# Attention output products ahead of the raw scores, and the queries' rotation in two pieces

## The chip, the cores and the metric

The program runs on one core of a Trainium2 chip. TensorE does the matrix products (PE in the profile; its weight loads are PEld), VectorE (DVE) the elementwise work and maxima, ScalarE (ACT) exponentials and copies out of PSUM, GpSimd (POOL) elementwise work in SBUF, SyncE (SP) issues DMAs. The metric is the device time of one execution in microseconds (us), the median of several.

## The reference

Four layers on x of 8 sequences x 256 tokens x 128 features, each `x = x + layer(layernorm(x))`: attention with rotary embedding ("rope"), a transformer block with a mixture of experts ("ffn"), attention whose scores are a covariance plus a variance term ("cov"), and the same ffn block again. All attentions have 16 heads of 8 features. Cut to its core:

```
rope: q, k, v = rot(x Wq.T + bq), rot(x Wk.T + bk), rot(x Wv.T + bv)
      out = unrot(softmax(q k.T / sqrt(8)) v) Wo.T + bo
cov:  softmax((q - mean(q)) (k - mean(k)).T / 8 + var(q) var(k).T / 8) v Wo.T
ffn:  h = x + attention(layer_norm(x)); h + moe(layer_norm(h)), top 2 of 8 experts, hidden 512
rot(x1, x2) = [x1 cos - x2 sin, x1 sin + x2 cos]      x1, x2: even and odd features
```

All data is float32.

## The kernel before, in words

Everything stays in SBUF. The two halves of the program (ph 0 and 1) each take two layers: first an attention pipeline over 16 items, an item being one sequence in one layer (rope then ffn in ph 0, cov then ffn in ph 1), then `mixture`, the experts over all tokens.

The pipeline goes in steps. In one step each engine works on up to six items that stand at different stages, called u, t, a, m, n, p from the oldest to the youngest. n is projected to queries, keys and values, and these are turned to feature-major (`do_zT`, `do_proj`, `do_kT`, `do_qT`). m gets its raw scores, `do_raw` (line 370), two heads at a time, of which VectorE takes the row maxima (`do_max`, line 982); the maxima are turned (`do_mT`, line 394) and sent by DMA into a spare row of the turned queries as a shift. a gets the shifted scores the other way round, `do_scores` (line 357), of which ScalarE takes the exponentials (`do_exp`, line 729), and the products of these with the values, `do_pv` (line 384). t's output is turned (`do_outT`, line 454), divided on VectorE (`divide`, lines 992 and 996), for rope rotated back on GpSimd, turned and multiplied by Wo. u is normalised and turned for the gate (`do_uT`, line 482).

A step on TensorE has eight slots, 0 to 7. Slot i has `do_scores` of heads 2i and 2i+1 of a, then `do_raw` of heads 2i-2 and 2i-1 of m, then transposes or other small products, then a `do_pv`. The order of each engine's instructions is that of the code; engines meet at semaphores alone. I write S for a `do_scores` of two heads, R for a `do_raw` of two heads, PV for a `do_pv`.

The features of four heads lie on the 128 partitions, 32 to a head, so a score product of head h uses only the 32 rows of TensorE's array at 32 * (h % 4): a strip. Heads 2i and 2i+1 of a slot's S are on two strips, and the R beside it, one pair of heads behind, is on the other two. PV uses all rows but 32 columns of the array for each of four heads.

S and the transposes write into a ring of four banks that ScalarE empties, R and the projections into a ring of three banks that VectorE empties. An R has to wait until the maxima of the heads three ring places before are taken; S for exponentials; `do_pv(g, ..)` for all four exponentials of the group g.

On VectorE a rope item n is rotated by two products for each of keys (1), queries (0) and values (2): `rotate` (lines 966 and 967), with the order of the calls written out in `step`. GpSimd adds the two products (`rotated`, line 1280) and lays keys and queries out for the transposes (`stack_k`, `stack_q`).

Of the kernel before, what the change touches and what calls it, by code (L numbers as in the profile page):

```python
# [7 lines left out]
ALU = mybir.AluOpType  # L8
# [95 lines left out]
def build(nc, d, out):  # L104
    ctx = ExitStack()
    with ctx:
        def sb(name, shape, dt=F32):
            return ctx.enter_context(nc.sbuf_tensor(name, shape, dt))
# [10 lines left out]
        def event(name, per):  # L119
            return Event(sem(name), per)  # L120
# [24 lines left out]
        ropeA = sb("ropeA", [P, 3, TT, H, HD])  # L145
        ropeB = sb("ropeB", [P, 3, TT, H, HD])
# [9 lines left out]
        QKV = sb("QKV", [P, 3, TT, D])  # L156
        R1 = sb("R1", [P, 3, TT, H, HD])
        R2 = sb("R2", [P, 3, TT, H, HD])
# [60 lines left out]
        roped = event("roped", {"rope": 6})  # L219
# [56 lines left out]
        def dve_bank(*key):  # L276

            return bankR[:, ring_r.place[key]]
# [63 lines left out]
        def _(pe):  # L342
# [6 lines left out]
            def do_scores(layer, b, i):  # L349

                if i % 4 == 0:
                    need(pe, shifted[i // 4], layer, b)
                for h in (2 * i, 2 * i + 1):
                    ring_e.take(pe, ("S", layer, b, h))
                    rows, kb, g = head_rows(layer, b, h)
                    for z in range(TT):
                        k = mm(act_bank("S", layer, b, h)[:, z * T:z * T + T], KT[rows, kb, g, z * P:z * P + P],  # L357
                               QT[rows, kb, g, :], start=True, stop=True)
                    k.then_inc(scores.sem, 1)
                    ring_e.give(("S", layer, b, h), exped, layer, b, h + 1)  # L360
# [14 lines left out]
            def do_pv(layer, b, g, kc):  # L375
                need(pe, exped, layer, b, HG * g + HG)
                if (g, kc) == (0, 0):
                    need(pe, stacked, layer, b)
                    need(pe, pv_copied, layer, b, 0)
                if (g, kc) == (2, 0):  # L380
                    need(pe, pv_copied, layer, b, 1)
                cols = slice((g // 2) * T, (g // 2) * T + T)
                for j in range(HG):
                    k = mm(bankO[SL * j:SL * j + SL, cols], Vx[:, b % VB, kc, HG * g + j, :],  # L384
                           Pr[:, g % 2, j, kc, :], start=(g % 2 == 0 and kc == 0),
                           stop=(g % 2 == 1 and kc == TT - 1))
                if kc == TT - 1:
                    k.then_inc(pv.sem, 1)
# [117 lines left out]
            def step(u, t, a, m, n, p):  # L506
                if a:
                    do_scores(*a, 0)
                    do_raw(*a, 7)
                if n:  # L510
                    do_zT(*n)
                if t:
                    do_pv(*t, 3, 0)

                if a:
                    do_scores(*a, 1)
                if m:
                    do_raw(*m, 0)
                if a:
                    do_mT(*a, 1)  # L520
                if t:
                    do_pv(*t, 3, 1)
                if n:
                    do_proj(*n)

                if a:
                    do_scores(*a, 2)
                if m:
                    do_raw(*m, 1)
                if a:  # L530
                    do_pv(*a, 0, 0)

                if a:
                    do_scores(*a, 3)
                if m:
                    do_raw(*m, 2)
                if t:
                    do_outT(*t)
                if m == (0, 0):
                    do_fold()  # L540
                if a:
                    do_pv(*a, 0, 1)

                if a:
                    do_scores(*a, 4)
                if m:
                    do_raw(*m, 3)
                if u:
                    do_uT(*u)
                if a:  # L550
                    do_pv(*a, 1, 0)

                if a:
                    do_scores(*a, 5)
                if m:
                    do_raw(*m, 4)
                if n and LAYERS[n[0]] != "rope":
                    do_kT(*n)
                if a:
                    do_pv(*a, 1, 1)  # L560

                if m:
                    do_mT(*m, 0)
                if a:
                    do_scores(*a, 6)
                if m:
                    do_raw(*m, 5)
                if u:
                    do_gate(*u)
                if t:  # L570
                    do_onT(*t)
                if n:
                    if LAYERS[n[0]] == "rope":
                        do_kT(*n)
                    else:
                        do_qT(*n)
                if a:
                    do_pv(*a, 2, 0)

                if a:  # L580
                    do_scores(*a, 7)
                if m:
                    do_raw(*m, 6)
                if t:
                    do_wo(*t)
                if n and LAYERS[n[0]] == "rope":
                    do_qT(*n)
                if a:
                    do_pv(*a, 2, 1)
# [300 lines left out]
        def _(dve):  # L890
            v = nc.vector
            tt = v.tensor_tensor
# [53 lines left out]
            def rope_operands(ap):  # L946
                half = ap.rearrange("p n (w o) -> p n w o", o=2)
                n = ap.shape[1]
                ev = half[:, :, :, 0].unsqueeze(2).broadcast_to([P, n, 2, HD // 2])
                od = half[:, :, :, 1].unsqueeze(2).broadcast_to([P, n, 2, HD // 2])  # L950
                return ev, od

            def flat(ap):
                return ap.rearrange("p c t h (u w) -> p (c t h) u w", u=2)

            def heads(ap):

                return ap.rearrange("p c t (h x) -> p (c t h) x", x=HD)

            def rotate(layer, b, c):  # L960

                need(dve, proj_copied, layer, b)
                if (layer, b, c) == (0, 0, 1):
                    dve.wait_ge(in_rope2, 4 * 16)
                ev, od = rope_operands(heads(QKV[:, c:c + 1]))
                tt(flat(R1[:, c:c + 1]), ev, flat(ropeA[:, c:c + 1]), ALU.mult).then_inc(roped.sem, 1)
                tt(flat(R2[:, c:c + 1]), od, flat(ropeB[:, c:c + 1]), ALU.mult).then_inc(roped.sem, 1)  # L967

            def turn(layer, b, part):
                if LAYERS[layer] == "cov":  # L970
# [8 lines left out]
            def do_max(layer, b, i):  # L979
                for h in (2 * i, 2 * i + 1):  # L980
                    need(dve, raw, layer, b, h + 1)
                    v.tensor_reduce(M[:, b % 2, :, h], dve_bank("raw", layer, b, h).rearrange("p (t k) -> p t k", t=TT),  # L982
                                    AX.X, ALU.max, negate=True).then_inc(maxed.sem, 1)
# [49 lines left out]
            def step(gone, u, t, a, m, n, nxt):  # L1033
                if a:
                    do_max(*a, 7)
                if m:
                    do_max(*m, 0)
                rope = n and LAYERS[n[0]] == "rope"
                if n:
                    do_proj(*n)  # L1040
                if m:
                    do_max(*m, 1)
                if n:
                    turn(*n, 0)
                if rope:
                    rotate(*n, 1)
                if m:
                    do_max(*m, 2)
                if n:
                    turn(*n, 1)  # L1050
                if rope:
                    rotate(*n, 0)
                if t:
                    divide(*t)
                if m == (0, 0):
                    do_fold()
                if m:
                    do_max(*m, 3)
                if m:
                    do_max(*m, 4)  # L1060
                if u:
                    rest_of_u(*u)
                if nxt:
                    norm_in(*nxt)
                if m:
                    do_max(*m, 5)
                if rope:
                    rotate(*n, 2)
                if u:
                    do_gate(*u)  # L1070
                if block_of(gone) is not None:
                    weigh(*block_of(gone))
                if block_of(u) is not None:
                    choose(*block_of(u))
                if m:
                    do_max(*m, 6)
                if t:
                    residual(*t)
                    norm3_in(*t)
# [419 lines left out]
```

## Time and profile before

| | |
|---|---|
| Time before, median of 3 runs | 1014.32 us (1014.15, 1014.32, 1019.89) |
| Profiled execution, its own time | 1015.21 us |
| Its span in the trace | 1013.4 us |
| Busy in the span | PE 96%, PEld 72%, ACT 60%, DVE 56%, POOL 37% |
| Matmuls | 8418 |
| Mean granted TensorE clock, share of full | 0.984 |

The span is the stretch of the trace from the first instruction to the last; the profiled execution took 1.81 us more than its span. A busy share of PE counts matmuls whose ends are modelled, overlapping ones included. Times in the trace count from the start of the span.

### The profile page before, as it was taken

Reading aid. Unit: us, or ns where it says so; the run is one execution under the profiler, and the core shown is the slowest. Engines: PE = TensorE matmul, PEld = TensorE weight load, DVE = VectorE, ACT = ScalarE, POOL = GpSimd, SP = SyncE. Lnnn points to the kernel's source line nnn. Section 1 sums busy time; section 2 is a strip of 40 time slices with the busy share of each in tenths; the row PEclk is TensorE's granted clock in tenths of the full one; section 3 lists DMA queues with packets and bytes.
Section 4 is the critical chain, followed back from the end, with each engine's and each line's share of the span. In section 5 each row is a group of like instructions: output and inputs, shape, how many; then the busy total and the mean of one; then the engine's idle time right before and its main releaser. Section 6 shows DMA issues by size and latency. Waiting matters only on the chain.

```text
span 1013.4 us, 22026 instructions
## 1 busy us (share of the span) xinstructions
PE 970.4 (96%) x8418; PEld 731.9 (72%) x8418; DVE 563.2 (56%) x1434; ACT 604.5 (60%) x1144; POOL 374.1 (37%) x797
## 2 busy tenths in 40 slices
PE   2989999999999999999999999999999999999998
PEld 2655556666557999999886666666665799999997
DVE  4797887888982221222336878788898222121211
ACT  1376668878787444444355777787878745444343
POOL 6768777657721100013112446366771110000000
PEclk9998889999999999999999999999999999999999
DMA  9000000000000000000000000000000000000000
GB/s 287 9 3 2 3 2 3 3 3 3 3 3 2 1 2 1 1 1 1 2 1 2 3 3 3 3 3 3 3 3 3 2 1 12 1 11 2 7 6 11
DMA packets 9960, 10.42 MB, mean 10 GB/s; under 512 B 1528, under 2 KB 7552, under 8 KB 9856
## 3 DMA queue, kind: packets, MB, share of 16 engines
q1 hardware_dynamic: 8848, 7.64, 2.6%
q10 hardware_dynamic: 1008, 1.38, 0.5%
q8 instruction: 68, 1.11, 0.4%
q14 instruction: 36, 0.29, 0.1%
HBM read 7.44 MB, written 1.05 MB: 8 GB/s over the span
## 4 chain that ended last, share of the span: by engine, by line
PE 78%; DVE 17%; issue 2%; POOL 1%; DMA 0%; ACT 0%; DVEq 0%; ACTq 0%; POOLq 0%
PE bankR L613 23%; PE bankO L384 10%; DVE M L982 8%; PE bankE L403 8%; PE bankE L602 6%; PE bankE L357 6%; PE bankE L604 6%; PE bankE L603 6%; PE bankR L370 3%; DVE QKV L944 2%; PE bankE L394 2%; PE bankR L454 1%; PE bankR L424 1%; PE bankR L472 1%; DVE R L967 1%
## 5 line engine op out<-in xcount | busy, mean ns | idle before, releaser
L982 DVE TENSOR_REDUCE M<-bankR 128x2 f32<-128x512 f32 x512 | 326.3, 684 | 70.2 <-PE bankR L370 68.4
L729 ACT ACTIVATE Pr<-bankE 128x512 f32<-128x512 f32 x512 | 276.9, 594 | 108.1 <-PE bankE L357 105.8
L839 ACT ACTIVATE Pr<-bankE,b1c 128x512 f32<-128x512 f32 x256 | 171.1, 687 | 175.4 <-PE bankE L604 174.2
L1138 DVE SCALAR_TENSOR_TENSOR X<-bankR,WE,X 128x128 f32<-128x128 f32 x256 | 72.1, 344 | 327.5 <-PE bankR L613 327.5
L613 PEld LDWEIGHTS bankR<-w,Pr 128*128 128x128 f32 x2048 | 238.3, 192 | 6.3 <-issue 1.1
L613 PE MATMUL bankR<-w,Pr 128*128 128x128 f32 x2048 | 238.9, 276 | 0.9 <-DVE X L1138 0.9
L370 PE MATMUL bankR<-KQ 32*128 32x256 f32 x1024 | 170.4, 340 | 10.6 <-DVE On L996 3.7
L384 PE MATMUL bankO<-Pr,Vx 128*32 128x256 f32 x2048 | 166.1, 398 | 0.6 <-ACT OT L721 0.3
L357 PEld LDWEIGHTS bankE<-KQ 32*128 32x128 f32 x1024 | 81.0, 188 | 96.0 <-issue 61.8
L357 PE MATMUL bankE<-KQ 32*128 32x256 f32 x1024 | 134.4, 334 | 0.0
L370 PEld LDWEIGHTS bankR<-KQ 32*128 32x128 f32 x1024 | 109.5, 192 | 23.3 <-DVE M L982 12.9
L602 PE MATMUL bankE<-THL,w1h 128*128 128x512 f32 x256 | 106.9, 417 | 0.0
L604 PE MATMUL bankE<-THL,w1l 128*128 128x512 f32 x256 | 101.1, 395 | 0.0
L603 PE MATMUL bankE<-THL,w1h 128*128 128x512 f32 x256 | 100.9, 394 | 0.0
L1222 POOL TENSOR_SCALAR lnsmall<-meanvar 128x2 f32<-128x2 f32 x48 | 10.9, 228 | 236.2 <-DVE meanvar L912 233.7
L721 ACT ACTIVATE KQ<-bankE 128x512 fp32r<-128x512 f32 x128 | 70.8, 604 | 24.2 <-PE bankE L403 23.9
L384 PEld LDWEIGHTS bankO<-Pr,Vx 128*32 128x32 f32 x2048 | 41.1, 109 | 35.4 <-issue 12.0
L1297 POOL CAST Kst<-QKV 128x512 fp32r<-128x512 f32 x24 | 16.2, 674 | 134.3 <-DVE QKV L942 93.0
L604 PEld LDWEIGHTS bankE<-THL,w1l 128*128 128x128 f32 x256 | 48.1, 188 | 11.9
L602 PEld LDWEIGHTS bankE<-THL,w1h 128*128 128x128 f32 x256 | 48.3, 189 | 10.2
L603 PEld LDWEIGHTS bankE<-THL,w1h 128*128 128x128 f32 x256 | 48.3, 189 | 8.7
L403 PE MATMUL bankE<-ident_r,Kst 128*128 128x256 f32 (+1 forms) x256 | 43.0, 319 | 4.1 <-POOL Kst L1300 4.1
(157 smaller groups left out, 1137.3 us busy)
## 6 DMA issues: line engine op xcount, KB each, us to landing
THL<-in_w SPq DMA_DIRECT2D x1, 2048.0 KB, 9.1
KQ<-MT SPq DMA_DIRECT2D x128, 4.0 KB
X<-in_x SPq DMA_DIRECT2D x8, 128.0 KB, 7.3
out_x<-X SPq DMA_DIRECT2D x4, 256.0 KB, 2.3
ropeA<-in_ropeA ACTq DMA_DIRECT2D x1, 384.0 KB, 5.9
ropeB<-in_ropeB ACTq DMA_DIRECT2D x1, 384.0 KB, 6.0
w_lo_rope<-in_w_qkv_rope ACTq DMA_DIRECT2D x1, 192.0 KB, 3.0
b_qkv_rope<-in_b_qkv_rope ACTq DMA_DIRECT2D x1, 192.0 KB, 4.9
```

The costliest lines, as they stand in the source:

```text
L357: k = mm(act_bank("S", layer, b, h)[:, z * T:z * T + T], KT[rows, kb, g, z * P:z * P + P], QT[rows, kb, g, :], start=True, stop=True)
L370: k = mm(dve_bank("raw", layer, b, h)[:, z * T:z * T + T], QT[rows, kb, g, z * P:z * P + P], KT[rows, kb, g, :], start=True, stop=True)
L384: k = mm(bankO[SL * j:SL * j + SL, cols], Vx[:, b % VB, kc, HG * g + j, :], Pr[:, g % 2, j, kc, :], start=(g % 2 == 0 and kc == 0), stop=( ...
L403: return mm(bank[:, i * P:i * P + n], src, ident_r[:, 0:n], start=True, stop=True)
L602: mm(acc, w1h[:, e, w], th, start=True, stop=False)
L603: mm(acc, w1h[:, e, w], tl, start=False, stop=False)
L604: mm(acc, w1l[:, e, w], th, start=False, stop=True).then_inc(hid.sem, 1)
L613: k = mm(dve_bank("out", ph, at)[:, t * D:t * D + D], G[:, e % 2, c, t * P:t * P + P], w2[:, e * FC + c, :], start=(c == 0), stop=(c == FC ...
L729: nc.scalar.activation(Pr[:, (h // HG) % 2, h % HG], act_bank("S", layer, b, h).rearrange("p (k q) -> p k q", k=TT), ACT.Exp, scale=EXP_SC ...
L839: nc.scalar.activation(G[:, e % 2, c, :], act_bank("hid", ph, at, c), ACT.Gelu_apprx_tanh, bias=b1c[:, e * FC + c:e * FC + c + 1]).then_in ...
L982: v.tensor_reduce(M[:, b % 2, :, h], dve_bank("raw", layer, b, h).rearrange("p (t k) -> p t k", t=TT), AX.X, ALU.max, negate=True).then_in ...
L1138: v.scalar_tensor_tensor(xt[:, j, t, :], dve_bank("out", ph, at)[:, t * D:t * D + D], WE[:, j * BT + t, e:e + 1], xt[:, j, t, :], ALU.mult ...
```

## The change

On TensorE, in slots 2 to 5 of each step, `do_pv` of item a is issued directly behind `do_scores`, and so ahead of `do_raw` of item m and of the transposes. On VectorE, `rotate` now does one of its two products per call; keys' and values' two products stay together where they were, while the queries' two go apart: the first behind `do_max(m, 3)`, the second behind `do_max(m, 4)`, where before both stood ahead of `divide` and `do_max(m, 3)`. The instructions on ScalarE and SyncE stay in their order, and so do those of GpSimd.

```diff
@@ TensorE, step
                 if a:
                     do_scores(*a, 2)
+                if a:
+                    do_pv(*a, 0, 0)
                 if m:
                     do_raw(*m, 1)
-                if a:
-                    do_pv(*a, 0, 0)
 
                 if a:
                     do_scores(*a, 3)
+                if a:
+                    do_pv(*a, 0, 1)
                 if m:
                     do_raw(*m, 2)
...
@@ VectorE
-            def rotate(layer, b, c):
+            def rotate(layer, b, c, x):
 
                 need(dve, proj_copied, layer, b)
                 if (layer, b, c) == (0, 0, 1):
                     dve.wait_ge(in_rope2, 4 * 16)
-                ev, od = rope_operands(heads(QKV[:, c:c + 1]))
-                tt(flat(R1[:, c:c + 1]), ev, flat(ropeA[:, c:c + 1]), ALU.mult).then_inc(roped.sem, 1)
-                tt(flat(R2[:, c:c + 1]), od, flat(ropeB[:, c:c + 1]), ALU.mult).then_inc(roped.sem, 1)
+                own, table = ((R1, ropeA), (R2, ropeB))[x]
+                tt(flat(own[:, c:c + 1]), rope_operands(heads(QKV[:, c:c + 1]))[x], flat(table[:, c:c + 1]),
+                   ALU.mult).then_inc(roped.sem, 1)
...
@@ VectorE, step
                 if n:
                     turn(*n, 1)
-                if rope:
-                    rotate(*n, 0)
                 if t:
                     divide(*t)
                 if m == (0, 0):
                     do_fold()
                 if m:
                     do_max(*m, 3)
+                if rope:
+                    rotate(*n, 0, 0)
                 if m:
                     do_max(*m, 4)
+                if rope:
+                    rotate(*n, 0, 1)
                 if u:
                     rest_of_u(*u)
```

The order that results on TensorE, slots 2 to 5 of the first step in which item t exists, before (S is line 357, R 370, PV 384, the transposes of `do_outT` 454, of `do_mT` 394):

```order
L357 MATMUL bankE<-KQ 128x256 x4
L370 MATMUL bankR<-KQ 128x256 x4
L384 MATMUL bankO<-Pr,Vx 32x256 x4
L357 MATMUL bankE<-KQ 128x256 x4
L370 MATMUL bankR<-KQ 128x256 x4
L454 MATMUL bankR<-ident,OT 128x128 x4
L384 MATMUL bankO<-Pr,Vx 32x256 x4
L357 MATMUL bankE<-KQ 128x256 x4
L370 MATMUL bankR<-KQ 128x256 x4
L384 MATMUL bankO<-Pr,Vx 32x256 x4
```

The same place now:

```order
L357 MATMUL bankE<-KQ 128x256 x4
L384 MATMUL bankO<-Pr,Vx 32x256 x4
L370 MATMUL bankR<-KQ 128x256 x4
L357 MATMUL bankE<-KQ 128x256 x4
L384 MATMUL bankO<-Pr,Vx 32x256 x4
L370 MATMUL bankR<-KQ 128x256 x4
L454 MATMUL bankR<-ident,OT 128x128 x4
L357 MATMUL bankE<-KQ 128x256 x4
L384 MATMUL bankO<-Pr,Vx 32x256 x4
L370 MATMUL bankR<-KQ 128x256 x4
```

PV has moved from behind R to between S and R; each R now has a PV ahead of it and the next slot's S (or transposes) behind it.

VectorE in a rope step with an item t, from the rotation of the keys on, before (line 982 the maxima, 966 and 967 the rotation products, 992 and 996 the division, 909 and 912 the statistics of the next item):

```order
L966 TENSOR_TENSOR R<-QKV,ropeA 128x256
L967 TENSOR_TENSOR R<-QKV,ropeB 128x256
L982 TENSOR_REDUCE M<-bankR 128x2 x2
L966 TENSOR_TENSOR R<-QKV,ropeA 128x256
L967 TENSOR_TENSOR R<-QKV,ropeB 128x256
L992 RECIPROCAL rden<-bankR 128x32
L996 TENSOR_TENSOR On<-bankR,rden 128x4x32 x2
L982 TENSOR_REDUCE M<-bankR 128x2 x4
L909 BN_STATS stats<-X 128x6 x2
L912 BN_AGGR meanvar<-stats 128x2 x2
```

The same place now (both products of `rotate` have line 966):

```order
L966 TENSOR_TENSOR R<-QKV,ropeA 128x256
L966 TENSOR_TENSOR R<-QKV,ropeB 128x256
L982 TENSOR_REDUCE M<-bankR 128x2 x2
L992 RECIPROCAL rden<-bankR 128x32
L996 TENSOR_TENSOR On<-bankR,rden 128x4x32 x2
L982 TENSOR_REDUCE M<-bankR 128x2 x2
L966 TENSOR_TENSOR R<-QKV,ropeA 128x256
L982 TENSOR_REDUCE M<-bankR 128x2 x2
L966 TENSOR_TENSOR R<-QKV,ropeB 128x256
L909 BN_STATS stats<-X 128x6 x2
```

The division and the maxima of slot 4 moved ahead of the queries' products, and each of these stands behind a pair of maxima.

## Rows read from the trace of the kernel before

**Rows 1.** The page's first part: busy time, share and count by engine.

```profile
PE 970.4 (96%) x8418; PEld 731.9 (72%) x8418; DVE 563.2 (56%) x1434; ACT 604.5 (60%) x1144; POOL 374.1 (37%) x797
```

**Rows 2.** Stretches of steps: length, busy PE, PEld, DVE, ACT, POOL, then clock, DMA.

```profile
62.99:160.88 97.89, 91.64 (x844) 56.49 (x840) 80.88 (x164) 64.83 (x131) 75.82 (x135) 0.86 0.01 2
160.88:223.15 62.27, 61.41 (x677) 38.33 (x673) 51.81 (x109) 50.33 (x106) 41.05 (x88) 1.00 0.01 3
223.15:289.42 66.27, 64.98 (x705) 41.43 (x701) 58.23 (x155) 52.42 (x115) 43.33 (x98) 1.00 0.01 3
...
557.88:643.34 85.46, 83.55 (x845) 52.19 (x841) 70.25 (x141) 63.52 (x131) 46.85 (x114) 0.98 0.01 3
```

**Rows 3.** TensorE, slots 2 to 5, ffn item n, no u: start, us, instruction, idle.

```profile
193.19 0.39 PE L357 MATMUL bankE<-KQ 32*128 32x256 f32 x2
...
193.42 0.28 PE L357 MATMUL bankE<-KQ 32*128 32x256 f32 x2
...
193.88 0.64 PE L384 MATMUL bankO<-Pr,Vx 128*32 128x256 f32 x8
194.45 0.39 PE L357 MATMUL bankE<-KQ 32*128 32x256 f32 x2
...
195.25 0.63 PE L454 MATMUL bankR<-ident,OT 128*128 128x128 f32 x4 [0.19 <-DVE M L982]
...
196.38 0.39 PE L357 MATMUL bankE<-KQ 32*128 32x256 f32 x2
...
197.41 0.39 PE L357 MATMUL bankE<-KQ 32*128 32x256 f32 x2
...
198.23 1.15 PE L403 MATMUL bankE<-ident_r,Kst 128*128 128x256 f32 x8
...
199.87 0.27 PE L394 MATMUL bankE<-ident,M 128*8 128x128 f32 x1
```

**Rows 4.** TensorE where no item m is left: S stands alone.

```profile
305.89 0.50 PE L357 MATMUL bankE<-KQ 32*128 32x256 f32 x4
306.32 0.44 PE L482 MATMUL bankE<-ident,U 128*128 128x128 f32 x2
306.69 0.64 PE L384 MATMUL bankO<-Pr,Vx 128*32 128x256 f32 x8
```

**Rows 5.** TensorE, slots 2 to 5 of an ffn step with an item u.

```profile
240.97 0.39 PE L357 MATMUL bankE<-KQ 32*128 32x256 f32 x2
...
247.65 0.38 PE L394 MATMUL bankE<-ident,M 128*8 128x128 f32 x2
```

**Rows 6.** VectorE in the last rope step.

```profile
142.50 1.29 DVE L982 TENSOR_REDUCE M<-bankR 128x2 f32<-128x512 f32 x2
...
146.66 0.63 DVE L966 TENSOR_TENSOR R<-QKV,ropeA 128x256 f32<-128x256 f32 x1
...
148.09 0.34 DVE L992 RECIPROCAL rden<-bankR 128x32 f32<-128x32 f32 x1
...
148.87 2.48 DVE L982 TENSOR_REDUCE M<-bankR 128x2 f32<-128x512 f32 x4
```

**Rows 7.** TensorE in the same step, slot 5 and behind it.

```profile
149.01 1.39 PE L370 MATMUL bankR<-KQ 32*128 32x256 f32 x4 [0.55 <-DVE On L996]
...
151.34 0.59 PE L394 MATMUL bankE<-ident,M 128*8 128x128 f32 x2
```

**Rows 8.** TensorE in a cov step: start of slot 2, and behind slot 5.

```profile
575.96 0.39 PE L357 MATMUL bankE<-KQ 32*128 32x256 f32 x2
...
583.97 0.38 PE L394 MATMUL bankE<-ident,M 128*8 128x128 f32 x2
...
584.30 0.39 PE L370 MATMUL bankR<-KQ 32*128 32x256 f32 x2
```

**Rows 9.** VectorE in the same cov step.

```profile
576.57 1.29 DVE L982 TENSOR_REDUCE M<-bankR 128x2 f32<-128x512 f32 x2
...
584.90 1.29 DVE L982 TENSOR_REDUCE M<-bankR 128x2 f32<-128x512 f32 x2 [0.66 <-PE bankR L370]
```

More of the change, by code:

```diff
@@ L530, in step @@
                 if a:
-                    do_pv(*a, 0, 0)
+                    do_scores(*a, 3)
                 if a:
-                    do_scores(*a, 3)
+                    do_pv(*a, 0, 1)
                 if m:
@@ L541, in step @@
                 if a:
-                    do_pv(*a, 0, 1)
+                    do_scores(*a, 4)
                 if a:
-                    do_scores(*a, 4)
+                    do_pv(*a, 1, 0)
                 if m:
@@ L550, in step @@
                 if a:
-                    do_pv(*a, 1, 0)
+                    do_scores(*a, 5)
                 if a:
-                    do_scores(*a, 5)
+                    do_pv(*a, 1, 1)
                 if m:
@@ L558, in step @@
                     do_kT(*n)
-                if a:
-                    do_pv(*a, 1, 1)
                 if m:
@@ L1045, in step @@
                 if rope:
-                    rotate(*n, 1)
+                    rotate(*n, 1, 0)
+                    rotate(*n, 1, 1)
                 if m:
@@ L1067, in step @@
                 if rope:
-                    rotate(*n, 2)
+                    rotate(*n, 2, 0)
+                    rotate(*n, 2, 1)
                 if u:
```

## The prediction

> **What bounds the kernel now.** I read the page first: TensorE is busy 96% of the span, no other engine over 60% [rows 1]. That share alone proves little, since matmuls overlap in it, so I then cut the attention pipeline at the projections of successive steps [rows 2]. The four stretches of the rows are 5 rope steps (97.89 us, 19.58 each), 4 steps that load an ffn item but have no item u (62.27, 15.57 each), 4 with both (66.27, 16.57 each), and 5 cov steps (85.46, 17.09 each). The second half of the program repeats the two ffn kinds in the same number, and each half ends with one further step with u and m. In the ffn steps TensorE is busy nearly throughout at full clock and VectorE has 3 us free in each: (62.27 - 51.81) / 4 = 2.6. In the rope steps the mean clock is 0.86, VectorE is busy 80.88 of 97.89, and TensorE is seen waiting: an R of slot 5 stands idle until the division is done [rows 7]. So ffn steps are set by how long TensorE's own blocks take, rope steps by VectorE in slots 3 to 5, and cov steps stand between.
>
> **What a slot costs on TensorE.** This is the view on which I rest most. In slot 2 of an ffn step S starts at 193.19 and PV at 193.88; PV then takes until 194.45, which is 0.57 [rows 3]. S and R together, eight products, so take 0.69, and in slot 4, where nothing waits, 197.41 - 196.38 - 0.57 = 0.46. Where no item m is left and S stands alone with half as many products, it takes 306.32 - 305.89 = 0.43 [rows 4]. R beside S is thus almost free, 0.03 us. The reason can be seen in the starts: S's second pair of products starts 0.23 behind its first pair [rows 3], one pair on two strips, the next on the same two strips once the first is through. R uses the other two strips in the same 0.46. The change puts PV, which uses all rows, between S and R. And the S that now follows R without anything between is that of the next slot: R has heads 2i-2 and 2i-1, S heads 2i+2 and 2i+3, four apart, so on the same two strips as R. That pair goes one behind the other. I cost every S and every R of slots 2 to 5 at 0.43 of its own.
>
> The Trainium skill, TensorE: Matmul & The Clock Gate, Part 3, says that a weight load overlaps running matmuls only where it goes to another row group; by that rule the trace agrees, in the 0.23 between products of one strip. TensorEngine Tiling (Array Packing), Key Properties, has the rule that a change of tiling mode drains the array. Read as the only cost of the new order, it would charge for one or two more mode changes in a step and not for the lost company on the strips, a few tenths of a microsecond per step; that would be the second rival below.
>
> **ffn steps.** Before, the S and R blocks of slots 2 to 5 take, waits included, 0.69, then 195.25 - 194.45 = 0.80, then 0.46, then 198.23 - 197.41 = 0.82: 2.77 in all [rows 3]. After, eight blocks of 0.43 are 3.44. The four PVs, the transposes of the output and of the keys are the same in number and cost. Per step that is +0.67. The stretch with an item u is as long, 247.65 - 240.97 = 6.68 [rows 5] against 199.87 - 193.19 = 6.68 [rows 3], though it holds a transpose more, 306.69 - 306.32 = 0.37 [rows 4]. Its S and R blocks are then 2.77 - 0.37 = 2.40, and the change costs it 3.44 - 2.40 = +1.04. There are 4 steps of the first kind in each half and 5 of the second (4 and the last with an m): 8 x 0.67 + 10 x 1.04 = 5.4 + 10.4 = +15.8 us. Counted in this are the waits which the new order takes away: of R for a bank in slots 2, 3 and 5, together 2.77 - 4 x 0.46 = 0.93, now covered by PV. The cover holds if VectorE keeps up. An R now reaches an idle VectorE 1.00 (S and PV) + 0.60 (from the start of R to the maxima, 584.90 - 584.30 [rows 8, 9]) = 1.60 into slot 2, where before the maxima began at 576.57 - 575.96 = 0.61 [rows 8, 9]. VectorE is 1.0 later there, but TensorE's slots have grown by as much two slots on, and its 2.6 us of free time is enough. I add nothing; a bound is the whole 0.99 once per step, which would make these terms 18 x 0.99 = 18 us dearer, but nothing in the rows points to more than a tenth or two.
>
> **cov steps.** Here VectorE is at work without a gap from slot 2's maxima to behind slot 5's: its next wait is ahead of the maxima of slot 6 [rows 9]. So its 1.0 us later start goes through to the last R of slot 5, and to the keys' transposes behind it. The transposes of the maxima, 583.97 before [rows 8], then come 0.98 later, less the 0.57 of a PV that no longer stands ahead of them: +0.41. Six such steps (the five of the rows and one ahead of them) make +2.5. Bounds: -0.5 per step if VectorE had slack that I don't see, +1.0 if the PV saves nothing.
>
> **rope steps.** In the row's step the maxima of slot 2 start at 142.50, the queries' products at 146.66, the division at 148.09, the maxima of slots 4 and 5 at 148.87, and the transposes of the maxima at 151.34 [rows 6, 7]. Now the maxima of slot 2 start 0.98 later (as above), but the queries' two products, 148.09 - 146.66 = 1.43, are gone from ahead of the division. So division at 147.64 and slot 4's maxima at 148.42; two maxima take half of the four's 2.4, so they are through at 149.6, and the transposes of the maxima can follow at 149.7, 1.65 earlier. What is given back: the first of the queries' products, some 0.45, now lies ahead of slot 5's maxima, on which the R of slot 6 waits. The second ends near 151.7, where GpSimd had both by 148.1; but GpSimd is busy rotating the output back then, and the queries are transposed only in slot 7, so I price that at nothing, and at 0.5 if GpSimd is late. That leaves 1.2 per step for the five steps with a t, -6.0. Shorter waits also mean fewer stretches at half clock. A mean of 0.86 [rows 2] means that 28% of the 97.89 us, 27 us, ran at the 1.2 GHz level; on TensorE's path alone full clock would give back half of that, 13.7, but much of it lies in waits on VectorE. I take 2.5. Rope together: -8.5, between +5 (1.0 later per step, and nothing won by the moved products) and -15. The first rope steps, which lack an a or a t, I leave at nothing.
>
> **The sum.** 15.8 + 2.5 - 8.5 = +9.8, against the profiled execution's 1015.2: 1025.0. The median before is 0.9 lower, so by difference 1024.1; with a tenth per ffn step for VectorE's lateness I say 1025. The mixture stages have no slot of this kind, and get nothing.
>
> **The rivals.** (1) The rope steps gain nothing: VectorE's later start in slot 2 cancels the moved products and the clock falls as before. For it: VectorE's 80.88 busy of 97.89, and the price of 1.0 per step is sure. Against it: 1.43 leaves the chain in which TensorE is seen to wait. Time: 1015.2 + 18.3 + up to 3 = 1033 to 1036. (2) The strips cost nothing, PV in front of R hides R's waits and only those show: faster. Then R and the next S share 0.46 as before, the stretch of slots 2 to 5 has six blocks of about 0.45, 2.7 against 2.77 and 2.40, some +2.4 over the 18 ffn steps; with the rope gain of 8.5 to 15 and cov at 0 to 2.5 the end is 1003 to 1010. It decides if two products on one strip could overlap; their 0.23 distance speaks against it. (3) The rope gain is whole, with the clock at full: -13 to -15 there, 1018 to 1021. For it: each low-clock stretch follows a wait that gets shorter. (4) VectorE becomes the bound of the ffn steps as well, by several tenths per step: 1030 to 1040. The 2.6 us free speak against it. That the change doesn't do what it says can be left out: the order of both engines shows it.
>
> **How the numbers follow.** Forecast (1021 to 1030) 0.50, rival 1 with the upper part of the sum 0.18, rival 3 0.20, rival 4 0.06, rival 2 0.06. The range 1017 to 1035 leaves out rival 2 and the ends of 1 and 4. A difference under 1%, 10.1 us, counts as none that can be told, so slower begins at 1024.5, near the middle of the forecast: 0.30 of its 0.50, all of rivals 1 and 4, 0.54; faster only by rival 2, 0.06; the same 0.40.
>
> **What would show it.** In the changed profile an S of slots 2 to 5 alone should take 0.43 to the PV, an R followed by S 0.86 to 0.88; ffn steps should be 16.2 to 16.3 and 17.6 long, cov steps 17.2, rope steps 17.5 to 18.5 with a clock above 0.86. VectorE's first maxima should start 1.6 into slot 2. The prediction is wrong if R with the next S takes under 0.6, or if rope steps stay at 19.6.

## The result and the profile after

The changed kernel takes 1033.84 us (median of 4, 1029.37 to 1035.05) against 1017.11 us of the kernel before on the same chips (median of 4, 1014.15 to 1020.18): ratio 1.0168, 95% interval 1.0136 to 1.0199. The profiled execution took 1032.67 us, its span 1030.9, which is 17.5 over the span before.

The first part of the page, as [rows 1]:

```profile
PE 990.2 (96%) x8418; PEld 745.2 (72%) x8418; DVE 563.9 (55%) x1434; ACT 604.2 (59%) x1144; POOL 373.9 (36%) x797
```

TensorE's share is 96% as before, though the kernel is slower: busy time holds matmuls that go one behind the other where they went side by side. Stretches between projections of successive steps, columns as in [rows 2]: five rope steps, four ffn steps without u, three of the steps with u, the five cov steps.

```profile
62.82:157.48 94.66, 89.64 (x844) 56.14 (x841) 81.64 (x164) 64.78 (x131) 72.58 (x127) 0.91 0.01 2
157.48:223.52 66.04, 64.52 (x677) 40.14 (x673) 52.43 (x109) 49.65 (x106) 42.83 (x93) 1.00 0.01 3
223.52:276.15 52.63, 51.76 (x532) 33.03 (x529) 43.84 (x114) 40.07 (x87) 36.70 (x85) 1.00 0.01 3
564.73:651.24 86.51, 83.84 (x844) 52.11 (x841) 69.74 (x141) 61.83 (x131) 46.62 (x112) 1.00 0.01 3
```

An ffn step without u takes 66.04 / 4 = 16.51 where it took 15.57, one with u 52.63 / 3 = 17.54 where it took 16.57: +0.94 and +0.97. The five cov steps together are 1.05 longer, the five rope steps 3.2 shorter [rows 2].

TensorE in an ffn step of the second half without u, as [rows 3], from the S of slot 3 to slot 6; up to the keys' transposes (line 403) each row is a block:

```profile
670.28 0.40 PE L357 MATMUL bankE<-KQ 32*128 32x256 f32 x4
670.61 0.64 PE L384 MATMUL bankO<-Pr,Vx 128*32 128x256 f32 x8
671.18 0.55 PE L370 MATMUL bankR<-KQ 32*128 32x256 f32 x4
671.91 0.63 PE L454 MATMUL bankR<-ident,OT 128*128 128x128 f32 x4 [0.19 <-DVE M L982]
672.47 0.50 PE L357 MATMUL bankE<-KQ 32*128 32x256 f32 x4
672.90 0.64 PE L384 MATMUL bankO<-Pr,Vx 128*32 128x256 f32 x8
673.47 0.51 PE L370 MATMUL bankR<-KQ 32*128 32x256 f32 x4
673.81 0.40 PE L357 MATMUL bankE<-KQ 32*128 32x256 f32 x4
674.14 0.64 PE L384 MATMUL bankO<-Pr,Vx 128*32 128x256 f32 x8
674.71 0.54 PE L370 MATMUL bankR<-KQ 32*128 32x256 f32 x4
675.19 1.15 PE L403 MATMUL bankE<-ident_r,Kst 128*128 128x256 f32 x8
...
676.49 0.45 PE L357 MATMUL bankE<-KQ 32*128 32x256 f32 x2
...
677.13 0.41 PE L464 MATMUL bankE<-ident,On 128*128 128x128 f32 x2
677.64 1.11 PE L403 MATMUL bankE<-ident_r,Qst 128*128 128x256 f32 x8
```

Three things are to be seen. S alone takes 672.90 - 672.47 = 0.43, as forecast. R with the next slot's S takes 674.14 - 673.47 = 0.67: more than 0.46 side by side, less than the 0.86 of two blocks apart. And slot 3's R, 671.18, lasts 0.73 to the transposes of the output, which wait for the maxima of slot 2's R. Slot 6, whose order is that of before, is longer: S and R 677.13 - 676.49 = 0.64, then 0.51 to the queries' transposes. The like step of this half in the trace before, from the keys' transposes on:

```profile
665.14 1.15 PE L403 MATMUL bankE<-ident_r,Kst 128*128 128x256 f32 x8
666.22 0.64 PE L384 MATMUL bankO<-Pr,Vx 128*32 128x256 f32 x8
...
667.10 0.39 PE L357 MATMUL bankE<-KQ 32*128 32x256 f32 x2
...
667.55 0.44 PE L464 MATMUL bankE<-ident,On 128*128 128x128 f32 x2
667.74 1.22 PE L403 MATMUL bankE<-ident_r,Qst 128*128 128x256 f32 x8
```

There slot 6 was 0.45 and 0.19, and a PV stood between the keys' transposes and it.

### The profile page after: what moved, and what is told of

The parts are those of the page before. It is cut to its first block, busy times and chain, and to the rows that moved or that the text cites. A ratio compares the mean times of both kernels' runs of the same rounds, so it can differ in the third digit from the quotient of the medians.

```text
span 1030.9 us, 22027 instructions
## 1 busy us (share of the span) xinstructions
PE 990.2 (96%) x8418; PEld 745.2 (72%) x8418; DVE 563.9 (55%) x1434; ACT 604.2 (59%) x1144; POOL 373.9 (36%) x797
## 3 DMA queue, kind: packets, MB, share of 16 engines
HBM read 7.44 MB, written 1.05 MB: 8 GB/s over the span
## 4 chain that ended last, share of the span: by engine, by line
PE 82%; DVE 13%; issue 2%; POOL 1%; ACT 0%; DMA 0%; ACTq 0%; DVEq 0%; POOLq 0%
PE bankR L613 22%; PE bankO L384 10%; DVE M L982 9%; PE bankE L403 8%; PE bankE L357 7%; PE bankE L602 6%; PE bankE L604 6%; PE bankE L603 6%; PE bankR L370 5%; PE bankR L424 2%; PE bankE L394 2%; PE bankR L454 1%; PE bankR L472 1%; PE bankR L426 1%; PE bankR L425 1%
## 5 line engine op out<-in xcount | busy, mean ns | idle before, releaser
L370 PE MATMUL bankR<-KQ 32*128 32x256 f32 x1024 | 159.3, 339 | 5.7 <-DVE M L982 3.4
L370 PEld LDWEIGHTS bankR<-KQ 32*128 32x128 f32 x1024 | 99.7, 191 | 64.9 <-issue 37.5
L357 PE MATMUL bankE<-KQ 32*128 32x256 f32 x1024 | 130.2, 323 | 0.0
L1301 POOL CAST Kst<-QKV 128x512 fp32r<-128x512 f32 x24 | 15.8, 657 | 134.4 <-DVE QKV L942 92.2
L602 PEld LDWEIGHTS bankE<-THL,w1h 128*128 128x128 f32 x256 | 48.2, 188 | 10.2
```

What stands on the lines that cost most here:

```text
L370: k = mm(dve_bank("raw", layer, b, h)[:, z * T:z * T + T], QT[rows, kb, g, z * P:z * P + P], KT[rows, kb, g, :], start=True, stop=True)
L602: mm(acc, w1h[:, e, w], th, start=True, stop=False)
```

## The experiments

Ratios are to the kernel before on the same chip, with 95% intervals. "No-u" and "u" steps are the ffn steps without and with an item u, as above.

**1. TensorE's new order alone.** VectorE keeps the order of before; slots 3 to 5 are changed like slot 2:

```diff
                 if a:
                     do_scores(*a, 2)
+                if a:
+                    do_pv(*a, 0, 0)
                 if m:
                     do_raw(*m, 1)
-                if a:
-                    do_pv(*a, 0, 0)
...
```

> The new order on TensorE alone; VectorE keeps the old order. Theory A (S and R lose each other's company on the strips, 0.43 us per block, and VectorE starts 1.0 us later in slot 2): ffn steps 16.46 and 17.50 us long and cov steps 17.30, as with both parts; rope steps no better than before, 19.6 to 20.5; in all +21 to +27 us, ratio 1.021 to 1.027. Rival B (the cost comes from VectorE's new order): ffn steps as before, 15.5 and 16.57, ratio 1.00 to 1.005.

Measured 1043.03 us, ratio 1.0251 (1.0209 to 1.0293). The ffn step next to the rope part, in the columns of [rows 2]:

```profile
165.45:181.93 16.48, 16.13 (x172) 10.04 (x169) 12.91 (x27) 12.37 (x27) 11.87 (x25) 1.00 0.01 2
```

It is the changed kernel's 16.5, with VectorE's order untouched, and the cov steps take the changed kernel's 17.3. The cost is TensorE's. The five rope steps take 99.6 us, where the kernel before took 97.9 at the same mean clock of 0.86.

**2. VectorE's new order alone.** TensorE keeps its order:

```diff
-                if rope:
-                    rotate(*n, 0)
                 if t:
                     divide(*t)
...
                 if m:
                     do_max(*m, 3)
+                if rope:
+                    rotate(*n, 0, 0)
                 if m:
                     do_max(*m, 4)
+                if rope:
+                    rotate(*n, 0, 1)
...
```

> The new order on VectorE alone; TensorE keeps the old order. Theory A: ffn and cov steps to 0.05 us as before (15.51, 16.57, 16.84), rope steps 1 to 2 us shorter, in all -5 to -9 us, ratio 0.991 to 0.995. Rival B: slower, ratio 1.012 or more. Rival C (the moved products win nothing, because the queries come late): ratio 0.998 to 1.003.

Measured 1007.48 us, ratio 0.9897 (0.9856 to 0.9938). The ffn steps are those of before. The five rope steps take 90.91 us where they took 97.89 [rows 2], at clock 0.94:

```profile
60.24:151.15 90.91, 83.05 (x845) 51.21 (x841) 80.65 (x164) 64.00 (x131) 76.17 (x134) 0.94 0.01 2
```

This half of the change is a gain by itself, a little more than theory A had, and the two halves' ratios multiply to 1.0251 x 0.9897 = 1.0145, within the interval of both together. The same kernel once more, beside the last one of experiment 8:

> The VectorE part of the change alone, once more beside the run above on the same chip. Ratio 0.987 to 0.993; the five rope steps 88 us plus 0.36 per us at half clock, within 1.5 us.

1009.60 us, ratio 0.9938 (0.9913 to 0.9964). The intervals of the two overlap; the second missed the upper end of what was expected by a little.

**3. S and R on the same strips, nothing else.** The kernel before, with the raw scores' pairs swapped, in `do_raw` and likewise in the column of M in `do_max`:

```diff
-                    rows, kb, g = head_rows(layer, b, h)
+                    rows, kb, g = head_rows(layer, b, h ^ 2)
...
```

> The kernel before, in its own order, but the pairs of heads in the raw scores are taken in the order 1,0,3,2,5,4,7,6, so that R has the same two strips as the S beside it. Nothing else changes: same products, waits, banks, mode changes. Theory A: each S and R that stand together take 0.88 instead of 0.46, in eight slots of each step, less the waits that are covered: ffn step 15.5 to 18.0 to 18.9 us, in all +75 to +100 us. Rival D (what costs time is the change between row strips and column strips, not the strips' company): no change, within 3 us.

Measured 1053.39 us (two runs), ratio 1.0358 (1.0311 to 1.0406). Slot 4 of an ffn step:

```profile
205.46 0.50 PE L357 MATMUL bankE<-KQ 32*128 32x256 f32 x4
205.80 0.40 PE L370 MATMUL bankR<-KQ 32*128 32x256 f32 x4
206.12 0.42 PE L384 MATMUL bankO<-Pr,Vx 128*32 128x256 f32 x4
```

S and R take 0.66 where they took 0.46 [rows 3], in the same order and with the same neighbours. That the company on four strips is worth something is so shown, against rival D; that it is worth 0.20 to 0.22 and not 0.42 is what my expectation had wrong: R starts 0.34 behind S, not 0.45, and its second pair 0.12 behind its first. So a block that is split off behind PV costs 0.43, one that stays next to another on its own strips 0.23.

**4. One pair of raw scores moved to the other strips.** The changed kernel, where slot 2's R and slot 3's S then differ in strips (the column of M in `do_max` likewise):

```diff
-                    rows, kb, g = head_rows(layer, b, h)
+                    rows, kb, g = head_rows(layer, b, {2: 4, 3: 5, 4: 2, 5: 3}.get(h, h))
...
```

> The changed kernel, with the raw scores of head pairs 1 and 2 issued in swapped order, so that the R of slot 2 (now heads 4 and 5) and the S of slot 3 (heads 6 and 7) behind it lie on different strips. Nothing else changes. Theory A: that one joint block takes 0.46 instead of 0.88, 0.42 less in each of 30 steps: ffn steps 16.46 to 16.05 and 17.50 to 17.10, in all -10 to -12 us against the changed kernel, ratio to before 1.005 to 1.009. Rival D: as the changed kernel, 1.017.

Measured 1030.92 us, ratio 1.0132 (1.0095 to 1.0169). The ffn steps did not move (16.46 and 17.48). Slots 2 and 3:

```profile
194.47 0.39 PE L370 MATMUL bankR<-KQ 32*128 32x256 f32 x2
...
194.92 0.64 PE L384 MATMUL bankO<-Pr,Vx 128*32 128x256 f32 x8
195.49 0.77 PE L370 MATMUL bankR<-KQ 32*128 32x256 f32 x4
196.44 0.63 PE L454 MATMUL bankR<-ident,OT 128*128 128x128 f32 x4 [0.19 <-DVE M L982]
```

R and the next S now take 194.92 - 194.47 = 0.45 instead of 0.67, as theory A has it. But the R behind them lasts 0.95 instead of 0.73, since the transposes of the output wait for the same maxima. What was won was waited away to 0.01 us. In slots 2 and 3 the changed kernel is bound by VectorE's maxima, not by TensorE's blocks.

**5. PV ahead of R, S and R left together.** Slots 2 to 5 as PV, S, R, each like slot 2 here, with VectorE's new order:

```diff
                 if a:
-                    do_scores(*a, 2)
-                if a:
                     do_pv(*a, 0, 0)
+                if a:
+                    do_scores(*a, 2)
                 if m:
                     do_raw(*m, 1)
...
```

> VectorE's new order, and on TensorE slots 2 to 5 as PV, S, R: PV is ahead of R as in the change, but S and R stay together on four strips. Theory A2 (the change loses by splitting S from R and by starting R 1.0 us later in slot 2; hiding R's waits behind PV is worth little): against VectorE's order alone (ratio 0.990) 0 to -3 us, ffn steps 15.4 to 15.5 and 16.45 to 16.6, ratio 0.986 to 0.991. Rival E (any PV ahead of R makes VectorE late and costs by itself): ffn steps 0.3 to 0.6 longer, ratio 0.998 or more.

Measured 1031.18 us, ratio 1.0138 (1.0105 to 1.0171): the number is rival E's, and my theory A2 falls in this point. The no-u steps take 15.99 to 16.02 in the first half of the program and 15.83 to 16.02 in the second, the u steps 17.22 to 17.37. Behind the keys' transposes of a no-u step of the first half:

```profile
183.69 0.38 PE L394 MATMUL bankE<-ident,M 128*8 128x128 f32 x2
183.99 0.47 PE L357 MATMUL bankE<-KQ 32*128 32x256 f32 x2
...
184.66 0.41 PE L464 MATMUL bankE<-ident,O 128*128 128x128 f32 x2
185.28 1.14 PE L403 MATMUL bankE<-ident_r,Qst 128*128 128x256 f32 x8 [0.21 <-POOL Qst L1324]
```

Slots 2 to 5, which begin at 177.08 in that step, are no longer than before, 6.61 against 6.68 [rows 3]. The loss lies behind them, 0.67 and 0.62 in slot 6 where 0.45 and 0.26 stood: the same place as in the changed kernel, and not where rival E has it. In this step the last 0.2 ahead of the queries' transposes is a wait for GpSimd, which lays the queries out behind the rotation of the output, and so behind VectorE's division. In the second half, where nothing is rotated, most no-u steps take 15.83. Not all of the 1.4% is in the ffn steps: in the profiled execution the five rope steps took 98.2 us, and TensorE ran for 10 us of the first mixture at the 1.2 GHz level, where the kernel before ran it at full clock.

**6. Slot 5 back in the old order.** The changed kernel, slot 5 as S, R, keys' transposes, PV:

```diff
-                if a:
-                    do_pv(*a, 1, 1)
                 if m:
                     do_raw(*m, 4)
                 if n and LAYERS[n[0]] != "rope":
                     do_kT(*n)
+                if a:
+                    do_pv(*a, 1, 1)
```

> The changed kernel, but slot 5 in the old order S, R, keys' transposes, PV; slots 2 to 4 as changed. Theory H (the changed kernel's slot 6 waits 0.2 at its S and 0.3 ahead of the queries' transposes because no PV stands behind the keys' transposes any more, while ScalarE empties their banks): those two waits go back to 0.45 and 0.20, and S and R of slot 5 share strips again; ffn steps without u 16.46 to 15.65 to 15.85, with u 17.50 to 17.1 to 17.3; in all -9 to -13 us against the changed kernel, ratio 1.004 to 1.008. Rival I (slot 6 waits because VectorE or GpSimd is late from slots 2 and 3): the block in slot 6 stays at 0.65 and the gap ahead of the queries at 0.50; ffn steps without u not under 16.0, ratio 1.010 or more.

Measured 1049.97 us, ratio 1.0332 (1.0309 to 1.0355), the other way than theory H's sum. The no-u steps take 16.7 us, not 15.65 to 15.85, and the u steps 17.6. A no-u step:

```profile
693.26 0.50 PE L370 MATMUL bankR<-KQ 32*128 32x256 f32 x4
...
694.54 0.50 PE L370 MATMUL bankR<-KQ 32*128 32x256 f32 x2 [0.42 <-DVE M L982]
694.97 1.15 PE L403 MATMUL bankE<-ident_r,Kst 128*128 128x256 f32 x8
696.05 0.64 PE L384 MATMUL bankO<-Pr,Vx 128*32 128x256 f32 x8
```

Its mechanism holds in slot 6: with a PV behind the keys' transposes, slot 6's block is back at 0.45 and the gap ahead of the queries' transposes at 0.20. But slot 4's R, slot 5's S and slot 5's R now follow each other with no PV between them, and the last waits for maxima of the first: 1.71 us for the three. The cov steps take 20.3 us (five in 101.56 us, 15 more than in the changed kernel), with the mean clock at 0.83, and this is most of the loss against the changed kernel. The five steps, and the R of slot 5 in the first of them:

```profile
569.19:670.75 101.56, 96.95 (x844) 62.02 (x841) 69.74 (x141) 65.40 (x131) 46.33 (x114) 0.83 0.01 2
```

```profile
576.50 1.39 PE L370 MATMUL bankR<-KQ 32*128 32x256 f32 x4 [0.65 <-DVE On L996]
```

**7. Slot 2 back in the old order; and the new order in rope steps alone.** The changed kernel with slot 2 as S, R, PV:

```diff
-                if a:
-                    do_pv(*a, 0, 0)
                 if m:
                     do_raw(*m, 1)
+                if a:
+                    do_pv(*a, 0, 0)
```

> The changed kernel, but slot 2 in the old order S, R, PV; slots 3 to 5 as changed. Theory A2: the maxima of slot 2 start 0.6 into it instead of 1.5, the wait of the output's transposes for them (0.30 us in the changed kernel) goes, and S and R of slot 2 share a block: ffn steps 0.3 to 0.6 us shorter (16.46 to 15.9 to 16.15), cov steps 0.4 to 0.8 shorter; in all -10 to -16 us against the changed kernel, ratio 1.001 to 1.007. Rival G (VectorE's start in slot 2 does not matter, only the four split blocks do): a quarter of the loss, ffn steps 0.2 shorter, ratio 1.011 to 1.014.

Measured 1022.45 us, ratio 1.0051 (1.0031 to 1.0071). In time it is theory A2, 11 us under the changed kernel. By steps it is less than that. The no-u steps of the second half are 0.23 shorter (65.11 / 4 = 16.28 against 66.02 / 4 = 16.51), those of the first half only 0.08 (16.43 on average), the u steps up to 0.3, where 0.3 to 0.6 was expected; the cov steps are 0.52 shorter. The six rope steps with an item a gave 4.6 in the profiled executions, in part at other clocks.

```profile
643.49:708.60 65.11, 64.36 (x676) 40.15 (x672) 52.25 (x109) 49.61 (x106) 32.64 (x77) 1.00 0.01 3
```

With VectorE's new order everywhere and TensorE's in the steps that load a rope item:

```diff
+                rope = n and LAYERS[n[0]] == "rope"
...
+                if a and rope:
+                    do_pv(*a, 0, 0)
                 if m:
                     do_raw(*m, 1)
-                if a:
+                if a and not rope:
                     do_pv(*a, 0, 0)
```

> VectorE's new order; TensorE's new order only in the steps that load a rope item (6 with an item a), the old order in all others. Theory A2: ffn and cov steps as before (15.5, 16.57, 16.84), rope steps as in the changed kernel, in sum 5 to 7 us longer than with VectorE's order alone; ratio 0.994 to 0.998. Rival F (where TensorE waits for VectorE, PV in front of R is a gain, and only the other steps lose): ratio below 0.990, under that of VectorE's order alone.

1010.86 us, ratio 0.9950 (0.9924 to 0.9976): theory A2 by its range, though the intervals overlap with those of VectorE's order alone. The steps tell them apart. The third of the five rope steps ran at full clock in these kernels: it takes 17.36 us here and 17.35 in the changed kernel, 16.43 and 16.45 in the two runs of VectorE's order alone. Even where TensorE waits for VectorE most, PV in front of R is no gain but costs 0.9, as in the ffn steps.

**8. The rope steps.** Two executions for their profiles alone:

> The changed kernel once more, for the rope steps alone. Theory J (the five rope steps take about 88 us plus 0.36 us for each us at half clock in them, whatever the order; the orders differ in how much half clock they draw): the sum of the five steps lies within 1.5 us of 88 + 0.36 times the half-clock time of this run. Rival K (the orders differ in the waits themselves): the same 94.7 us as in the first profile however much half clock there is.

> The kernel before once more, for the rope steps alone. Theory J: the five rope steps take 88 us plus 0.36 us per us at half clock, within 1.5 us, as in the first profile (97.9 with 27.3 us at half clock). Rival K: at least 3 us above that line, since the waits of slots 4 and 5 are longer in this kernel.

Five rope steps each, the changed kernel first, the kernel before below:

```profile
62.90:157.33 94.43, 89.49 (x844) 56.09 (x840) 81.39 (x164) 64.71 (x131) 74.37 (x132) 0.91 0.01 2
```

```profile
63.38:162.41 99.03, 92.47 (x845) 56.55 (x841) 80.51 (x164) 64.94 (x131) 75.15 (x134) 0.84 0.01 2
```

A mean clock of 0.84 is 2 x 0.16 x 99.03 = 31.7 us at the 1.2 GHz level, and 88 + 0.36 x 31.7 = 99.4; for the changed kernel 17.0 us and 94.1. Both are within theory J's bound, but the second says little: the changed kernel drew as much of the lower level as in its first profile. The third test of the line broke it: experiment 2's second run has

```profile
61.20:154.45 93.25, 88.52 (x845) 53.30 (x841) 81.59 (x164) 64.68 (x131) 77.73 (x138) 0.85 0.01 2
```

where the line says 98.1. So the orders differ in their waits. How much they draw of the lower level is not theirs alone: VectorE's order by itself drew 11 us of it in one execution and 28 in the other. All profiled executions side by side, with the sum of the five steps cut where slot 6 begins:

| five rope steps, us | in all | up to slot 6 | from slot 6 on | mean clock |
|---|---|---|---|---|
| kernel before | 97.9 / 99.0 | 51.5 / 52.1 | 46.4 / 46.9 | 0.86 / 0.84 |
| TensorE's order alone | 99.6 | 50.4 | 49.2 | 0.86 |
| VectorE's order alone | 90.9 / 93.2 | 42.7 / 45.6 | 48.2 / 47.6 | 0.94 / 0.85 |
| changed kernel | 94.7 / 94.4 | 45.1 / 45.1 | 49.6 / 49.4 | 0.91 / 0.91 |

At about equal clock (0.86 and 0.85) VectorE's order is worth 4.6 us over the five steps, and TensorE's costs 1.8. Then the queries' two products both behind slot 5's maxima, TensorE as before:

```diff
-                if rope:
-                    rotate(*n, 0, 0)
                 if m:
                     do_max(*m, 4)
                 if rope:
+                    rotate(*n, 0, 0)
                     rotate(*n, 0, 1)
```

> VectorE's new order alone, with both of the queries' products behind the maxima of slot 5 (in the change the first stands ahead of them). Theory J2 (in the rope steps what the change moved away from slot 5 comes back as a wait of slot 6's R for the maxima of head 8, behind the first product, 1.1 to 1.8 us long with VectorE's order alone): slot 6's block gets 0.3 to 0.8 shorter, 6 rope steps -2 to -5 us against the order of the change on VectorE alone; ratio 0.985 to 0.989. Rival L (the queries become late for their transposes in slot 7, and the wait moves there): rope steps as long or longer, ratio 0.990 to 0.994.

1006.11 us, ratio 0.9916 (0.9885 to 0.9947), beside 0.9938 (0.9913 to 0.9964) for the order of the change: not told apart, and the ratio is in rival L's range. In the third rope step, at full clock in both, slot 6's block went from 1.12 to 0.61, as theory J2 has it. The first product took 0.49 in its new place, where it had taken 0.89 beside GpSimd's rotation of the output:

```profile
106.58 0.39 PE L357 MATMUL bankE<-KQ 32*128 32x256 f32 x2
...
107.19 0.44 PE L464 MATMUL bankE<-ident,O 128*128 128x128 f32 x2
```

## Why the prediction was wrong in size

The forecast was 1025, 10.7 above the median then known (1.05%); measured is 1.68%. The sign, the place and the reason (R split from S) held; the sum, +9.8, should have been +17.5 in the profiled execution. Of the 7.7 that are missing, 5.3 are in the rope term, 3.3 in the ffn steps with the halves' ends, and cov and the first steps give back 0.9. Of what I said would show it, S alone (0.43), the later maxima (1.54 into slot 2, 1.60 forecast) and the lengths of the u and cov steps came within a tenth or so. R with the next S did not (0.67, not 0.86 to 0.88), nor the no-u steps (16.5, not 16.2 to 16.3) and the rope steps (18.9, not 17.5 to 18.5).

**The rope term failed.** It stood at -8.5 and was -3.2 (-4.6 in the second pair of profiles, 94.43 against 99.03). Its parts were 1.65 per step won ahead of slot 6, some 0.45 given back behind it, and 2.5 in all for the clock. By the table of experiment 8 the way to slot 6 became 6.4 and 7.0 us shorter in the five steps, 1.3 to 1.4 each, and the way from there on 3.2 and 2.4 longer, 0.6 and 0.5 each. Nothing came on top for the clock, though its mean rose from 0.86 and 0.84 to 0.91: whatever that gave is already in these two numbers. The 2.5 is the largest part of what is missing in the first pair. VectorE in the first rope step at full clock of the changed kernel, as [rows 6], and TensorE from slot 2, with its slot 6:

```profile
104.83 1.29 DVE L982 TENSOR_REDUCE M<-bankR 128x2 f32<-128x512 f32 x2 [0.86 <-PE bankR L370]
...
109.88 0.88 DVE L966 TENSOR_TENSOR R<-QKV,ropeA 128x256 f32<-128x256 f32 x1
110.69 1.28 DVE L982 TENSOR_REDUCE M<-bankR 128x2 f32<-128x512 f32 x2
```

```profile
103.29 0.50 PE L357 MATMUL bankE<-KQ 32*128 32x256 f32 x4
...
110.02 0.38 PE L394 MATMUL bankE<-ident,M 128*8 128x128 f32 x2
110.33 0.39 PE L357 MATMUL bankE<-KQ 32*128 32x256 f32 x2
...
111.42 0.50 PE L370 MATMUL bankR<-KQ 32*128 32x256 f32 x2 [0.57 <-DVE M L982]
111.85 0.44 PE L464 MATMUL bankE<-ident,O 128*128 128x128 f32 x2
```

The transposes of the maxima come 6.73 after slot 2's start, where they came 9.46 after it (151.34 - 141.88) in the step of [rows 7], which is partly at the lower level. What comes back does so in slot 6: the second half of its R waits for the maximum of head 8, which stands behind a product of 0.88, and the block takes 111.85 - 110.33 = 1.52 where 0.45 is its cost: 1.07 given back in this step, not 0.45. I had the mechanism, but priced the product at 0.45, though [rows 6] show it at 0.63 beside GpSimd's work, and moved it next to GpSimd's rotation of the output, which runs from 109.03 to 111.35 in this step. Experiment 8 shows the wait and its cause. How much of the 3 to 5 us between the two kernels is the lower clock level and how much are waits stays open; the line that I tried failed in one of three tests.

**The ffn term was 3.3 us too low, with errors both ways.** Forecast were +15.8 us for 18 steps at 0.67 and 1.04. Measured are +0.94 and +0.97 per step, and +19.1 with the ends of the halves, where the last two u steps and the mixture grew by 2.8 us together and 2.1 was in the sum.

Too dear in it: a block next to another on the same strips, 0.43 in the sum, cost 0.23 to 0.24 (experiment 3, and the 0.67 of the changed kernel). I had read the 0.23 between the products of a strip as their distance wherever they stand, and as agreeing with a rule by which no weight load overlaps a product on its own strip. The 0.23 holds for the first two products of a block only. The third follows at 0.12, and its weight load starts together with the second product, on the same strip (both at 673.70 in the changed kernel's step above; the four loads of the S behind R):

```profile
673.70 0.31 PEld L357 LDWEIGHTS bankE<-KQ 32*128 32x128 f32 x4
```

Left out of it: the wait of 0.3 for the maxima in slot 3 ("I add nothing"; the bound of 0.99 stood beside it), shown by experiment 4. Left out too: 0.5 in slot 6 of no-u steps (0.2 at S and R, 0.3 ahead of the queries' transposes), for cover that PV gave them (experiments 5 and 6), less 0.2 that the transposes themselves ran shorter. I had written that a moved PV is the same in cost; I didn't ask what it covered where it stood.

What slot 6 waits for can be read from ScalarE's copies in the changed kernel's step above. In the ring of four banks the second head of S takes the place of the keys' first bank, the output's transposes that of the keys' second, and the queries' transposes that of the turned maxima:

```profile
675.90 1.09 ACT L721 ACTIVATE KQ<-bankE 128x512 fp32r<-128x512 f32 x2 [0.57 <-PE bankE L403]
...
677.14 0.36 ACT L721 ACTIVATE MT<-bankE 8x256 fp32r<-8x256 f32 x1
```

The keys' copies end at 676.99 and the output's transposes start at 677.13; the maxima's copy ends at 677.50 and the queries' transposes start at 677.64. GpSimd had laid these queries out by 672.49, so it is not what they wait for. No run tests the copies by themselves.

**The cov term** was sized right: +0.41 per step forecast, 17.30 against 16.84 measured. The five of [rows 2] differ by 1.05 only, since the last of those before ran partly at the lower level (18.11 us); in the second execution of the kernel before, at full clock, the five took 84.0, which is 2.5 less than the 86.51 of the changed kernel.

Rival 2 (strips free) is refuted by experiments 1 and 3, rival 3 (whole rope gain) by the profile. Rival 1's reason (VectorE's later start cancels much of the moved products' worth) was nearest to what happened in the rope steps; rival 4's (VectorE bounds ffn steps too, by some tenths) in slots 2 and 3. I held both for alternatives to the sum where each was a part of it. That the measured 1033.84 lies in rival 1's 1033 to 1036 is luck: it had no gain at all in the rope steps, where 3 to 5 us were won, and lacked what the ffn steps cost beyond the sum.

The drain of the Trainium skill, TensorEngine Tiling (Array Packing), Key Properties, explains none of the 0.20 of experiment 3, where the mode changes stay the same in number. In the change itself there is room for it. A block two products deep on each strip takes 0.43 [rows 4], one of four 0.67, so each product deeper costs 0.12, and 0.19 is left for a block whatever its depth. The changed no-u step has six such blocks in slots 2 to 5 where four stood. Without waits these blocks are 4 x 0.46 = 1.84 us before and 4 x 0.43 + 2 x 0.67 = 3.06 now. My estimate from these numbers is that of the 1.2 us between them 2 x 0.19 = 0.4 goes to the two additional blocks, and 0.8 to products that no longer run side by side. No run tells a drain from any other fixed cost of a block.

## What to carry to other kernels

Before a product is moved, ask what it stands beside and what it stands behind: here one move cost company on the array (0.2 to 0.4 us per block), made the next engine's input 0.9 us late, of which 0.3 came back as a wait, and uncovered waits of 0.2 and 0.3 behind the keys' transposes. The waits that it was to hide were 0.2 to 0.4. Try the parts of a change alone: half of this one is worth -0.6 to -1.0%, the other half costs +2.5%. An elementwise product's price depends on what GpSimd does beside it in the new place, so take it from the contended rows.

## What the runs showed of the hardware that I had not expected

Two score blocks of four products on the same two strips take 0.67 together, not twice 0.43: the second block's first pair starts 0.34 behind the first block's and its second pair 0.12 later, while within a first block the pairs are 0.23 apart.

In experiment 6 all five cov steps had a stretch at TensorE's 1.2 GHz level: 17.3 us at a granted clock of 1.00 in the changed kernel became 20.3 us at a mean clock of 0.83. Ahead of the stretch TensorE had stood idle for 0.65 us before slot 5's R. The no-u steps of the same run had an idle time of 0.42 us at the same place and stayed at 1.00. That the longer wait is the reason is likely but not tested apart.

The lower level also differs between executions of one kernel: VectorE's new order alone took its five rope steps in 90.9 us at a mean clock of 0.94 and in 93.2 at 0.85.
